# Gather and window attention of a layer in one block, with set-up on GpSimd and the first loads ahead of the last stores

## What is computed

```python
neigh = gather(feats, inds)                      # per method, B x N x 10 x C
gf = concatenate([broadcast(center), neigh - center], axis=-1)
allf = stack(per_method, axis=-1)[..., perm]     # 4 methods
x16 = allf.reshape(B * N, k, total).astype(float16)
scores = einsum('bihd,bjhd->bhij', qh, qh) / sqrt(32)
attn = softmax(scores, axis=-1)
out = einsum('bhij,bjhd->bihd', attn, qh)
fused = out @ W_lin.T + b_lin
h1 = lrelu(instance_norm(W_conv1 @ g1)); feats1 = h1.max(axis=-1)
```

## Time and profile before

| what | us |
|---|---|
| median of the three runs | 2311.38 |
| lowest, highest | 2309.77, 2312.67 |
| span of the profiled execution | 2306.2 |
| busy in it: DVE, PE, ACT, POOL | 1904.0, 1865.0, 1616.7, 1007.8 |

### The profile page before, as it was taken

The page is one execution under the profiler, slowest core; times in us unless marked ns, Lnnn a source line. Parts: engine busy times, 40 slices in busy tenths (PEclk is TensorE's granted clock), DMA queues, the critical chain, the costliest instruction groups (busy, mean ns, idle before and its releaser), DMA issues. The chain is left out here.

```text
span 2306.2 us, 99850 instructions
## 1 busy us (share of the span) xinstructions
PE 1865.0 (81%) x37528; PEld 1286.8 (56%) x37528; DVE 1904.0 (83%) x3658; ACT 1616.7 (70%) x3249; POOL 1007.8 (44%) x995
## 2 busy tenths in 40 slices
PE   0296665888888566499999998677999999999967
PEld 0023335777777344389999997343554544454432
DVE  6798986999999599689989987783888888888865
ACT  0299985888888699689999998456555555555532
POOL 0000006999999200178888886001434444444311
PEclk9997668999999666699999999799999999999979
DMA  2103766666565167655555552212322322222210
GB/s 59 14 1 89 165 163 141 123 122 123 122 123 121 32 157 166 157 110 109 107 105 110 108 105 53 93 28 67 92 83 73 91 74 81 79 85 82 61 56 19
DMA packets 435513, 216.09 MB, mean 94 GB/s; under 512 B 301259, under 2 KB 404843, under 8 KB 435304
## 3 DMA queue, kind: packets, MB, share of 16 engines
q1 hardware_dynamic: 430120, 210.73, 39.2%
q10 hardware_dynamic: 5312, 4.31, 0.8%
HBM read 161.97 MB, written 52.96 MB: 93 GB/s over the span
## 5 line engine op out<-in xcount | busy, mean ns | idle before, releaser
L865 PE MATMUL pQ<-QM,QX 128*128 128x64 f16 (+1 forms) x5760 | 531.5, 216 | 2.1 <-issue 2.1
L863 PE MATMUL pQ<-neigh_lo,QX 128*128 128x32 f16 (+1 forms) x5760 | 519.8, 188 | 2.1 <-issue 2.1
L863 PEld LDWEIGHTS pQ<-neigh_lo,QX 128*128 128x128 f16 x5760 | 494.9, 103 | 5.4 <-issue 2.8
L865 PEld LDWEIGHTS pQ<-QM,QX 128*128 128x128 f16 x5760 | 486.9, 104 | 1.8 <-issue 1.7
L961 POOL TENSOR_TENSOR Dm<-Sc,mx 128x450 f32<-128x450 f32 x384 | 365.8, 953 | 77.8 <-DVE mx L921 77.8
L968 POOL TENSOR_TENSOR Ap<-E,R 128x450 f32<-128x450 f32 x384 | 366.0, 953 | 67.9 <-DVE R L934 57.5
L998 ACT ACTIVATE Vs<-pQ 128x480 f32<-128x480 f32 (+1 forms) x384 | 295.6, 770 | 4.7 <-PE pH L891 3.0
L930 DVE STREAM_TRANSPOSE AT<-Ap 128x480 f32<-128x480 f32 x384 | 259.3, 675 | 33.4 <-PE pH L891 10.9
L1963 POOL TENSOR_TENSOR MT<-cb,decay 128x512 f32 (+1 forms) x128 | 164.0, 1302 | 247.4 <-PEq L1731 150.6
L1011 ACT ACTIVATE E<-Dm 128x450 f32<-128x450 f32 x384 | 224.1, 584 | 60.1 <-POOL Dm L961 60.0
L921 DVE TENSOR_REDUCE mx<-Sc 128x15 f32<-128x450 f32 x384 | 224.0, 583 | 15.2 <-ACT Sc L992 15.1
(11 more groups left out here) (362 smaller groups left out, 3584.5 us busy)
## 6 DMA issues: line engine op xcount, KB each, us to landing
QM<-scratch_q SPq DMA_DIRECT2D x192, 240.0 KB, 2.7
QX<-scratch_q SPq DMA_DIRECT2D x768, 60.0 KB, 2.5
scratch_q<-QT SPq DMA_DIRECT2D x120, 360.0 KB, 4.8
Wg<-in_in_proj SPq DMA_DIRECT2D x64, 256.0 KB, 2.7
Wh<-in_in_proj SPq DMA_DIRECT2D x64, 256.0 KB, 2.8
Wo<-in_out_proj SPq DMA_DIRECT2D x64, 256.0 KB, 2.6
W_s<-in_in_proj SPq DMA_DIRECT2D x16, 256.0 KB, 2.7
CT<-scratch_c SPq DMA_DIRECT2D x192, 11.2 KB, 2.2
```

What stands on the lines that cost most here:

```text
L863: nc.tensor.matmul(pQ[:, p, u // PB, o + 32:o + BW], qx[u], W["neigh_lo"][:, 0:O], start=False, stop=True, skip_group_check=True)
L865: last = nc.tensor.matmul(pQ[:, p, u // PB, o:o + BW], qx[u], qm[u], start=False, stop=True, skip_group_check=True)
```

## The change

One function, `windows_and_attention`, takes the place of the two. Both stages of a layer are now in one block: each engine runs `steps` for the gather and then `steps` for the attention, and there is one block end and one clearing for both.

1. **Memory is shared.** The tiles of the gather are used again by the attention: `Sc` lies over `fb`, `apart`, `t16` and `l16`; `Vs`, `Hs` and (layer 1) `AT` over `onehot`; `Dm`, `E` and `A` over the first two buffers of `QT`; `ext` and `cen` over `hmax2`, and `AT` of layer 2 over `hmax1`. The PSUM tiles of the gather are released, and `pQ` and `pH` take their place.
2. **GpSimd** does all zeroing of `CT` and `QX` and all 8 (16) copies into `QM`, right behind its zeroing of the pads. Then it waits for the last stores of `QT`'s first two buffers, zeroes `A` and goes on to the attention.
3. **SyncE** issues the windows of groups 0 to 7 between the gather's loop and its last four steps, when the first four batches are stored and the zeroes are there. It waits for the last stores of the gather at attention step 7. All stores are issued by SyncE.
4. **TensorE** waits between its two stages for the masks, GpSimd's copies, and the last `l16`, `cen` and `ext`. VectorE and ScalarE go on without a wait of their own. ScalarE loads the masks at the gather's start.
5. The source of the `QX` loads is seen as two rows of 480 instead of ten of 96.

```diff
-def steps(eng, step, T, U):
+def steps(eng, step, T, U, before_last=None):
...
     with eng.Fori(1, T // U) as i:
...
+    if before_last:
+        before_last()
     for s in range(T, T + U):
...
-        Sc = sb("Sc", [128, ND, GC])
-        Dm = sb("Dm", [128, ND, GC])
-        E = sb("E", [128, ND, GC])
...
+        Sc = small[:, 0:ND * GC].rearrange("p (k x) -> p k x", k=ND)
...
+        early = QT[:, 0:2, :, :].rearrange("p k g x -> p (k g x)").bitcast(F32)
+        Dm, E, A = (early[:, i * ND * GC:(i + 1) * ND * GC].rearrange("p (k x) -> p k x", k=ND) for i in range(3))
...
         @block.sync
-                    for m in range(M // 2 if late(b) else M):
+                    for m in range(M):
                         store_windows(sp, k3, r, m)
-            steps(sp, step, B, 4)
-            for k in range(4):
-                sp.wait_ge(q_out[k], QO * (B // 4) + QO)
+            def load_windows(k, r):
+                src = q16[:, k % SL // 2, bass.ds(pack(r, k), 1), :, :].rearrange("p q s x -> p (q s) x")
+                sp.dma_start(QM[:, k:k + 2, 0, :], src).then_inc(q_in[k // 2], 16)
+                for h in range(4):
+                    sp.dma_start(QX[32 * h:32 * h + 32, k:k + 2, :, h, :].rearrange("p g w x -> p (g w) x"),
+                                 src[32 * h:32 * h + 32, :, :].rearrange("p g (w x) -> p g (w x)", w=SUBS // RES))\
+                        .then_inc(q_in[k // 2], 16)
+            def first_windows():
+                for k in range(4):
+                    sp.wait_ge(q_out[k], 2 * QO)
+                sp.wait_ge(wide_zeroed, NQ // 2)
+                for k in range(0, U, 2):
+                    load_windows(k, 0)
...
+                if at(0) and isinstance(at(0)[0], int) and at(0)[0] == U - 1:
+                    for k in range(4):
+                        sp.wait_ge(q_out[k], QO * (B // 4) + QO)
+            steps(sp, gather_step, B, 4, first_windows)
+            steps(sp, step, T, U)
...
         @block.gpsimd
+            nc.gpsimd.memset(CT[:, :, :], 0.0).then_inc(ct_zeroed, 1)
+            for k in range(0, NQ, 2):
+                nc.gpsimd.memset(QX[:, k:k + 2, :, :, :].rearrange("p k w h x -> p (k w h x)").bitcast(F32), 0.0)\
+                    .then_inc(wide_zeroed, 1)
+            for k in range(NQ):
+                for c in range(1, SEG):
+                    nc.gpsimd.tensor_copy(wide(k, c), column(c)).then_inc(wide_ready, 1)
+            for k in range(2):
+                pool.wait_ge(q_out[k], QO * (B // 4) + QO)
+            nc.gpsimd.memset(A[:, :, :], 0.0).then_inc(a_zeroed, 1)
...
         @block.tensor
+            steps(pe, gather_step, B, 4)
+            pe.wait_ge(const_in, 32)
+            pe.wait_ge(wide_ready, NQ * (SEG - 1))
+            pe.wait_ge(l16_ready, B + 2)
+            pe.wait_ge(cen_ready, B + 2)
+            pe.wait_ge(ext_ready, B + 2)
+            steps(pe, step, T, U)
...
-            v.memset(QX[:, 0, :, :, :].rearrange("p w h x -> p (w h x)").bitcast(F32), 0.0).then_inc(zeroed[0], 1)
-            for k in range(NQ // 2):
-                for c in range(1, SEG):
-                    v.tensor_copy(wide(k, c), column(c)).then_inc(wide_ready, 1)
...
-            for k in range(NQ // 2, NQ):
-                for c in range(1, SEG):
-                    nc.scalar.activation(wide(k, c), column(c), ACT.Copy).then_inc(wide_late, 1)
```

More of the change, by code:

```diff
@@ L445, in steps, with windows_and_attention @@
             step(k, lambda lag, k=k: (i * U + (k - lag), i + (k - lag) // U))
+    if before_last:
+        before_last()
     for s in range(T, T + U):
         step(s % U, lambda lag, s=s: (s - lag, (s - lag) // U) if 0 <= s - lag < T else None)
-def gather_windows(nc, io, scratch, layer, O, feats, runs, perm, rank, fixed):
+def windows_and_attention(nc, io, scratch, layer, O, feats, runs, perm, rank, fixed, W, hmax, stat, field, turn):
+    T = B * GROUPS
+    SL = 128 // O
+    U = RV = 8
+    NQ = 8
+    ND = 4
+    NA = 2 * SL
+    SEG = 1 + O // 32
+    BW = 32 * SEG
+    PB = 512 // BW
+    NBK = -(-SUBS // PB)
+    H2 = EXT // 2
     with ExitStack() as ctx:
@@ L459, in sem @@
         def sem(name):
-            used.append(ctx.enter_context(nc.semaphore(name + "_gw" + layer)))
+            used.append(ctx.enter_context(nc.semaphore(name + "_wa" + layer)))
             return used[-1]
-        H2 = EXT // 2
         ident, rep, place = (fixed[name] for name in ("ident", "rep", "place"))
[L465 to L468, removed]
@@ L481, in gather_windows @@
+        pQ = ctx.enter_context(nc.psum_tensor("pQ" + layer, [128, 2, NBK, 512], F32))
+        pH = ctx.enter_context(nc.psum_tensor("pH" + layer, [128, 2, 512], F32))
+        pads_zeroed = sem("pads_zeroed")
         f_in = [sem("f_in0"), sem("f_in1")]
@@ L497, in gather_windows @@
         LATE = M * NT - HOT
-        SL = 128 // O
         QO = 16 * (M + 2)
         ZEROS = 6
+        const_in = sem("const_in")
+        wide_zeroed = sem("wide_zeroed")
+        a_zeroed = sem("a_zeroed")
+        ct_zeroed = sem("ct_zeroed")
+        wide_ready = sem("wide_ready")
+        q_in = [sem(f"q_in{k}") for k in range(NQ // 2)]
+        c_in = [sem(f"c_in{k}") for k in range(RV // 2)]
+        scores_out = sem("scores_out")
+        shifted = sem("shifted")
+        projected = sem("projected")
+        max_ready = sem("max_ready")
+        exped = sem("exped")
+        summed = sem("summed")
+        r_ready = sem("r_ready")
+        probs = sem("probs")
+        turned = sem("turned_p")
+        vs_ready = sem("vs_ready")
+        mixed = sem("mixed")
+        hmax_done = sem("hmax_done")
+        copied = sem("copied")
+        squared = sem("squared")
         ctx.callback(clear, nc, used)
@@ L566, in _ @@
+            steps(pool, step, T, U)
         @block.vector
@@ L572, in _, with gather_step @@
             dve.sem_inc(q_v, 4 * QV)
-            def step(k, at):
+            dve.sem_inc(turned, NA)
+            dve.sem_inc(hmax_done, 2)
+            def gather_step(k, at):
                 if at(0):
@@ L613, in _, with gather_step @@
             pe.sem_inc(gathered, 2)
-            def step(k, at):
+            pe.sem_inc(projected, NQ)
+            pe.sem_inc(mixed, RV // SL)
+            def gather_step(k, at):
                 if at(0):
@@ new lines, in hots @@
+            def hots(b, h, j0, j1):
+                if j0 == 0:
+                    distance(b, 0)
+                for j in range(j0, j1):
+                    if j + 1 < LATE:
+                        act.wait_ge(late_hot, b * LATE + max(j - 1, 0))
+                        distance(b, j + 1)
+                    act.wait_ge(apart_ready, b * LATE + (j + 1))
+                    nc.scalar.activation(onehot[:, h, HOT + j, :], apart[:, j % 3, :], ACT.Relu, scale=-1.0,
+                                         bias=unit[:, :]).then_inc(late_hot, 1)
@@ new lines, in gather_step @@
+            def gather_step(k, at):
+                if at(0):
+                    (b, i), h = at(0), k % 2
+                    if first(b):
+                        act.wait_ge(gathered, b + 1)
+                        hots(b, h, 0, 2)
+                    act.wait_ge(tokens_out, b + 1)
+                    act.wait_ge(gathered, b + 1)
+                    nc.scalar.activation(t16[:, h, :], ptok[:, h, 0:NT * C], ACT.Copy).then_inc(t16_ready, 1)
+                    if not first(b):
+                        act.wait_ge(late_hot, b * LATE)
+                        hots(b, h, 0, 2)
+                if at(1):
+                    (b, _), k1 = at(1), (k - 1) % 4
+                    act.wait_ge(gathered, b + 3)
+                    act.wait_ge(q_v, b * QV + QV)
+                    nc.scalar.activation(ext[:, k1, :].rearrange("p (e x) -> p e x", e=2), pext[:, k1 % 2, :, 0:H2],
+                                         ACT.Copy).then_inc(ext_ready, 1)
+                if at(0):
+                    (b, i), h = at(0), k % 2
+                    hots(b, h, 2, LATE)
+                    act.wait_ge(f_used, b + 3)
+                    act.wait_ge(q_out[k], i * QO + QO)
+                    act.wait_ge(q_v, b * QV + QV)
+                    for s0, n0, n1 in RUNS:
+                        nc.scalar.activation(cen16[:, k, s0:s0 + n1 - n0], pcen[:, h, n0:n1], ACT.Copy)
+                        last = nc.scalar.activation(cen[:, k, s0:s0 + n1 - n0], pcen[:, h, n0:n1], ACT.Copy)
+                    last.then_inc(cen_ready, 1)
```

375 lines of the change are left out of this document (128 added, 247 removed).

## The result

| | before | after |
|---|---|---|
| median of 4 runs, us | 2310.57 | 2446.77 |
| lowest, highest | 2306.80, 2312.67 | 2443.34, 2455.51 |
| span of the profiled execution | 2306.2 | 2441.6 |

The account below looks back on a forecast made before the run. ScalarE bounds the gather, TensorE and ScalarE layer 2's attention. 31.7 + 3.2 - 2.6 - 5.0 = 27.3 us off the 2306.2 span gives 2278.9; with 5.2 for the median, 2284.1; range 2274 to 2301.

Parts of the forecast that it names:

- steady attention steps that take another time than before: Sign that the forecast is wrong: steady attention steps change their time, which no part of the sum allows for.
- (c): Gather's first steps: VectorE/GpSimd lock with slow copies makes it slower; 2298 at 1.5 us a copy; chance 0.06 plus 0.05.
- part 1: Border of gather and attention: first maximum follows the last QT piece at once, 15.5 and 16.2 us, together 31.7 gained.
- part 2: Fill of the attention pipeline: third maximum comes sooner after the first, 1.0 and 2.2 us, together 3.2 gained.
- part 4: GpSimd's fills and copies in the gather hold up VectorE's one-hots: 2.3 + 2.7 = 5.0 us lost.
- part 3: SyncE's queue: GpSimd's zeroing of A costs nothing; group 8's loads stall 2.3 and 0.3 us, together 2.6 lost.
- the three causes: Stacked in the gaps between gather and attention: last stores, block end and next start, set-up with cold loads.
- the two chains: Pipeline fill, first to third maximum: 3.97 us, or 2.69 if ScalarE's table load slips ahead of the wait.
- Rival (b): SyncE's queue: the 20 early loads issue as slowly as stores, 1.0 us each, giving 2299; chance 0.11.
- rival (d): Seam between stages: some wait keeps early scores from starting early, only the clearing goes, about 2309; chance 0.04.
- Rival (a): Layer 2's gather: QT's subtractions block against GpSimd's copies too, 1.6 us more, 2285.6; chance 0.12.

Follow-up runs that it names:

- 32 increments: The changed kernel with 32 semaphore increments nobody waits for added on TensorE before the ranking stage, moving its later code: 2288.73 us, ratio 0.9902.
- the undone version: The changed kernel with 32 increments, but SyncE issues the windows of groups 0 to 7 after the gather's last stores: 2311.13 us.

## Why the prediction was wrong, point by point

**The step that failed** is the sum: it starts from the span of before and carries both attention loops over at their old time. The prediction named this among the things that would prove it wrong, "steady attention steps that take another time than before, which no part of this sum allows for", but gave it no chance and no price. The premise behind it, not written there, was that deleting a block end does nothing to TensorE's other code. It moves that code by 23 places. For a loop of 1552 instructions that decides between seven blocks and eight, and the price is 158 us (2446.8 less 2288.7). It breaks down by the row from 1020.00 to 1071.30, one period: 1520 matmuls. With 32 increments the same 51.3 us hold 51.30 us of busy time for 2078 matmuls, so 1520 take 37.5, two passes of 18.8. After has 10.4 idle (51.30 less 40.92), and 3.4 more of busy time (40.92 less 37.5) at a granted clock of 0.90 for 1.00. 13.8 in each of 11.5 periods is 159.

None of the prediction's rivals had it: its way to a slower kernel, (c), was the lock in the gather. Nothing in the profile of before shows the stall. What could have shown the risk are its 47 code packets in section 3, a loop of more than six blocks, and the compiled instructions counted on both sides of the edit.

**The other steps**, from the traces; layer 2's attention from the kernel with 32 increments, in which it takes 469.6 us (before 467.2):

| step | forecast | measured | rows of after |
|---|---|---|---|
| part 1, the gap | 31.7 | 32.0 | last piece of QT to 349.69, maximum at 349.60; 947.27, 947.18 |
| part 2, the fill | 3.2 | 3.8 | third maximum 2.99 after the first, 4.39 before; 3.19, 5.60 before |
| part 4, the gather | -5.0 | -2.1 | last piece of QT 0.98 later; 186.74 behind the last `hmax` for 185.65 |
| part 3, group 8 | -2.6 | -11.6 | what the attention lost, and part 2's gain with it: 5.4 + 1.4 in layer 1; 2.4 + 2.4 in layer 2 |
| sum | 27.3 | 22.1 | |

The sum of 22.1 is near to what the moved code gives, 21.9 (2310.58 less 2288.73); that they agree to 0.2 is luck. The stages behind the attention, which the change doesn't touch, took from 867 to 872 us from run to run, and the trace with 32 increments has 4.1 us more there than before. So the four parts describe the change, apart from the code, to within some 4 us.

**Part 1** was right in size and its reason half wrong: all but some 3 us of it is the loads ahead of the stores, as the undone version shows; the three causes did not add.

**Part 2** was right. The table load still stands behind the wait for the first shift, the longer of the two chains that I had weighed:

```profile
350.25 1.28 ACT L979 ACT_TABLE_LOAD   x1 [1.69 <-POOLq L699]
```

**Part 3** is the term that was mis-sized most. Its first half held: GpSimd's zeroing of `A` starts at 348.42, 0.4 behind the range that I had, and it is ready in time.

```profile
348.42 1.70 POOL L697 MEMSET QT<- 128x1920 f32 x1 [152.26 <-DMA scratch_q<-QT]
```

For group 8 I had counted four stores from the end of QT. Batch 14's four were still in the queue, so that the eight took until 357.64, at 1.37 us each where the earlier trace rows has 1.0; I took 353.7. The mean of 1.0 was misread as the price of a store. In a burst, before already, the first two take 0.3 to 0.5 us and the next up to 1.65; after, the last six of the eight took 1.4 to 1.8 each. The two loads of `CT`, 3.17 us, lay beside the landing. The data came 3.8 us later than I had it (17.4 from the end of QT, not 13.6), and TensorE wanted it at 359.6, 10.0 behind the first maximum, not 11.3. That is the 7.5 for 2.3. In layer 2 TensorE waits 2.3 us for `CT`, a term that the sum doesn't have, and 2.2 for `QX`. Rival (b) had the right queue and the wrong instructions: the 20 early loads took 12.2 us to issue, within the 9.2 to 14 forecast, the stores grew.

**Part 4** had the mechanism, and the price twice too high. One-hots and GpSimd's set-up at the start of layer 1's gather:

```profile
187.20 5.58 DVE L742 TENSOR_SCALAR onehot<-place,rank 128x576 f16<-128x576 f16 x5
...
191.36 4.81 POOL L694 COPY QM<-neigh_hi 128x480 f16<-128x480 f16 x8
...
192.88 4.03 PE L822 MATMUL pext<-onehot,small 128*32 128x288 f16 x64 [3.25 <-DVE onehot L742]
```

Five one-hots took 5.58 us (6.95 forecast), a copy 0.60 (0.7 taken). The matmuls start at 192.88 for 191.73, and the stage itself starts 0.33 later: 0.8 lost, not 2.3. (In this part of the forecast the 801.1 for the one-hots of layer 2 isn't worked out from its rows, and the 3.1 should be 3.0; neither moves the time.) Rival (c), copies of over 1.3 us, falls, with a median of 0.66 in layer 2; rival (d), that the change doesn't do what it says, falls with part 1. Rival (a) was right in its mechanism. In layer 2 the 16 copies last until 801.84 and meet QT's first subtractions (VectorE's next batch stands below it for comparison; then all 16 copies, shortest, median and longest ns):

```profile
796.85 6.78 DVE L754 TENSOR_TENSOR QT<-hmax 128x1710 f16<-128x1710 f32 x3
...
806.80 5.63 DVE L754 TENSOR_TENSOR QT<-hmax 128x1710 f16<-128x1710 f32 x3
```

```profile
L694 POOL COPY QM<-neigh_hi x16: 583/657/2290, 788.9 to 799.6; 128x480 f16<-128x480 f16 x16
```

A subtraction took 2.3 us for 1.9, and a copy up to 2.29 for 0.58, as if each waited for the other. The Trainium skill, SBUF — State Buffer, section Who interferes with whom, says just this of a VectorE instruction with two SBUF inputs and a GpSimd instruction that reads SBUF; the trace agrees. It came to 1.1 us, not the 2.1 (three copies of 0.7) that rival (a) had, and the part's loss of 2.1 us holds whatever of it wasn't covered.

## What to carry to other kernels

A loop has a place in the instruction stream, and an edit anywhere ahead of it moves it: where a long unrolled loop comes near to what its engine can hold, count its instructions before and after an edit, compare the packets of the instruction queue, and pad or shorten the body. When all engines slow down at once and the waits say "issue", look at the code before you look at the data. And when several causes lie in one gap, ask which ends last; they hide one another and don't add.

## What the hardware showed beyond that

The stall costs more than its idle time, through TensorE's clock. After, around one stall:

```profile
1006.00:1012.00 6.00, 6.00 (x269) 5.78 (x256) 5.56 (x13) 6.00 (x14) 4.87 (x7) 1.00 0.60 113
1013.00:1016.00 3.00, 0.00 (x0) 0.00 (x0) 2.39 (x5) 1.86 (x4) 2.09 (x3) 1.00 0.41 87
1016.00:1020.00 4.00, 0.00 (x0) 0.00 (x0) 0.00 (x0) 0.00 (x0) 0.65 (x1) 0.65 0.38 71
1020.40:1024.40 4.00, 3.98 (x135) 3.69 (x138) 0.72 (x2) 1.30 (x2) 0.02 (x1) 0.54 0.01 4
1024.80:1028.00 3.20, 3.20 (x66) 3.20 (x66) 1.87 (x6) 2.97 (x8) 1.48 (x2) 1.00 0.13 17
```

The granted clock is full (2.4 GHz) while TensorE stands, falls within the stall to 0.65, is 0.54, near the 1.2 GHz level, for the four microseconds after it, and full again from 1024.8; three matmuls of L842 take 0.56 us in it and 0.37 after it. A second such stretch, 0.50 from 1044.6 to 1047.9, comes later in the same period, with TensorE busy throughout; from 1000 to 1400 us the kernel before has 1.00 in the mean. From 1016 to 1020 no engine works but GpSimd for 0.65 us: four groups in flight are not enough cover for a stall of 7 us.

The loop that touches seven blocks, 1792 places, runs without one fetch from 1040 to 1200; the one that touches eight, 2048 places, fetches nine blocks in two passes. By the number of instructions that the Trainium skill, Runtime: NRT & Kernel Launch, section Instruction fetch mechanics, gives for TensorE, eight blocks would have room; here the trace doesn't agree. Why they have not, and why it is every second pass, stays open.
